# Two LSTM layers under each other, the fourth 18 steps behind instead of 19, with two gates in one sigmoid and the gate o summed apart in the last steps

## What is computed

```python
x = x + cond_layer(x)                  # x @ (base + rank-8 part of cond) + x
x = x + tanh(x @ W_ih.T + cond @ W_hh.T + b_hh + b_ih)
x = x + lstm(x, cond, L2_Wx, L2_Wh, L2_b)      # "third layer", L2 in the code
x = x + lstm(x, cond, L3_Wx, L3_Wh, L3_b)      # "fourth layer", L3 in the code

def step(h, c, xp_t):                  # xp = x @ Wx + b
    a = xp_t + h @ Wh                  # [2, 2048]
    i, f, o, g = sigmoid(a[0:512]), sigmoid(a[512:1024]), sigmoid(a[1024:1536]), tanh(a[1536:])
    c = f * c + i * g
    h = o * tanh(c)
```

## Time and profile before

| | us |
|---|---|
| median of 3 runs | 11900.81 |
| lowest, highest | 11899.27, 11900.91 |
| the profiled execution | 11900.05 |
| its span on the core | 11898.2 |

### The profile page before, as it was taken

The page is one execution under the profiler, slowest core; times in us unless marked ns, Lnnn a source line. Parts: engine busy times, 40 slices in busy tenths (PEclk is TensorE's granted clock), DMA queues, the critical chain, the costliest instruction groups (busy, mean ns, idle before and its releaser), DMA issues.

```text
span 11898.2 us, 435945 instructions
## 1 busy us (share of the span) xinstructions
PE 11828.7 (99%) x231604; PEld 2698.0 (23%) x100532; DVE 8509.1 (72%) x46342; ACT 3758.9 (32%) x24698; POOL 1418.6 (12%) x5238
## 2 busy tenths in 40 slices
PE   8999999999999999999999999999999999999999
PEld 5222222222222222222222222222222222222222
DVE  2677777777777777777777777777777777777776
ACT  2233333333333333333333333333333333333332
POOL 4011111111111111111111111111111111111110
PEclk9999999999999999999999999999999999999999
DMA  4000000000000000000000000000000000000000
GB/s 164 25 4 5 4 5 4 5 5 4 5 5 4 5 5 4 5 4 5 4 5 5 4 5 5 4 5 5 4 5 4 5 4 5 5 4 5 5 5 3
DMA packets 374546, 107.86 MB, mean 9 GB/s; under 512 B 349594, under 2 KB 357830, under 8 KB 372436
## 3 DMA queue, kind: packets, MB, share of 16 engines
q1 hardware_dynamic: 362372, 61.96, 2.8%
q0 software_dynamic: 3504, 11.56, 0.3%
q10 hardware_dynamic: 6560, 6.32, 0.2%
HBM read 62.98 MB, written 16.78 MB: 7 GB/s over the span
## 4 chain that ended last, share of the span: by engine, by line
PE 99%; DVE 0%; issue 0%; ACT 0%; POOLq 0%; POOL 0%; DVEq 0%
PE bank L80 89%; PE bank L874 7%; PE bank L518 1%; PE bank L531 1%; PE bank L484 0%; DVE gates_t L1055 0%; DVE gates_t L1062 0%; ACT gate_o L950 0%; DVE state L1085 0%; DVE state L1088 0%; DVE state L1081 0%; ACT tanh_c L952 0%; DVE pre L1068 0%; DVE pre L1061 0%; DVE g_fc L1065 0%
## 5 line engine op out<-in xcount | busy, mean ns | idle before, releaser
L80 PE MATMUL bank<-wh,state 128*6 128x512 bf16 x196608 | 11055.6, 379 | 20.8 <-DVE state L1088 20.8
L1054 DVE STREAM_TRANSPOSE gates_t<-bank 128x256 f32<-128x256 f32 x4096 | 1843.6, 450 | 2015.3 <-PE bank L80 2013.7
L80 PEld LDWEIGHTS bank<-wh,state 128*6 128x6 bf16 x65536 | 1568.1, 86 | 7400.5 <-issue 6498.0
L945 ACT ACTIVATE gate_if<-pre 128x8 f32<-128x8 f32 x4096 | 859.8, 210 | 7256.0 <-DVE pre L1059 7256.0
L1081 DVE TENSOR_TENSOR state<-gate_o,tanh_c 128x8 f32<-128x8 f32 x4096 | 688.2, 168 | 836.0 <-ACT tanh_c L952 811.2
L1062 DVE STREAM_TRANSPOSE gates_t<-bank 128x128 f32<-128x128 f32 x4096 | 1252.5, 306 | 0.0
L1055 DVE STREAM_TRANSPOSE gates_t<-bank 128x128 f32<-128x128 f32 x4096 | 1122.9, 274 | 0.0
L983 POOL TENSOR_TENSOR y<-x,state 128x8 f32<-128x8 f32 x2048 | 434.5, 212 | 5374.2 <-DVE state L1088 5374.2
L950 ACT ACTIVATE gate_o<-pre 128x8 f32<-128x8 f32 x4096 | 855.0, 209 | 642.8 <-DVE pre L1068 642.4
L983 POOL TENSOR_TENSOR x<-x1r,state 128x8 f32<-128x8 f32 x2048 | 434.5, 212 | 4961.2 <-DVE state L1088 4961.2
L952 ACT ACTIVATE tanh_c<-g_c 128x8 f32<-128x8 f32 x4096 | 854.7, 209 | 9.7 <-DVE g_c L1072 9.7
(11 more groups left out here) (124 smaller groups left out, 3490.6 us busy)
## 6 DMA issues: line engine op xcount, KB each, us to landing
w<-in_w SPq DMA_DIRECT2D x8, 2048.0 KB, 13.2
out<-y_rows SPq DMA_DIRECT2D x1020, 8.0 KB, 1.8
wx<-in_x SPq DMA_DIRECT2D x16, 512.0 KB, 5.4
x1p<-x_t_all SPq DMA_DIRECT2D x128, 64.0 KB, 2.6
x1r<-x_t_all SPq DMA_DIRECT2D x128, 64.0 KB, 2.6
x_t_all<-wx ACTq DMA_DIRECT2D x6, 1024.0 KB, 4.8
wx<-in_Wh POOLq DMA_DIRECT2D x8, 512.0 KB, 4.2
wx<-in_Wh POOLq DMA_DIRECT2D x16, 256.0 KB, 4.9
```

The source lines that it names most:

```text
L80: return pe.add_instruction(mybir.InstMatmult(name=nc.get_next_instruction_name(), engine=mybir.EngineType.PE, ins=[pe.lower_ap(moving), p ...
L945: act.activation(gate_if[l][:, 1, :, 1], pre[l][:, HB:2 * HB], ACT.Sigmoid).then_inc(S[l]["f"], 1)
L1054: dve.transpose(gates_t[l][:, 0:gf, NS * NB:], banked[:, 0:gf]).then_inc(s["trans_if"], 1)
```

## The change

It has three parts.

1. LAG is 18 instead of 19. ROWS_AT falls from 4 to 3 by its formula. In the first chunk where only the fourth layer is left (number 128), its first step of the chunk's data is now step 2, the one in which quarters 2 and 3 were turned; so `done_before` moves them to step 1 there, behind quarters 0 and 1, and GpSimd adds the biases ahead of the residual in that step, since the residual waits for the state that VectorE writes only after the turning.
2. ScalarE does the sigmoids of i and f in one activation of 16 elements; the semaphore f becomes `if`.
3. In chunks 128 and 129, where the fourth layer is alone, the matmuls are done twice over the blocks of rows: 48 of 384 columns for i, f and g into the layer's own bank, then 48 of 128 columns for o into the third layer's bank, with a semaphore mm_o for the second. VectorE transposes o from there and waits for mm_o first.

```diff
-LAG = CH + 2 + 1
+LAG = CH + 2
 ...
+        if self.number == NCH:
+            own = [(L3, -1, 2), (L3, -1, 3)]
+            found = [x for x in found if x not in own] + (own if s == 1 else [])
+        return found
+    def lone(self):
+        return self.number is not None and self.number >= NCH
+    def own_turned(self, s):
+        return self.number == NCH and s == 1
 ...
-                def matmuls(l):
-                    w = wh[l][:, :, :, :, :, :, :].rearrange("p h k j s m c -> p h k j s (m c)")
+                def matmuls(l, to=None, first=0, last=NMS):
+                    to = gates[l][:, 0:NMS * C] if to is None else to
+                    w = wh[l][:, :, :, :, :, first:last, :].rearrange("p h k j s m c -> p h k j s (m c)")
 ...
-                            matmuls(l).then_inc(S[l]["mm"], 1)
+                            if t.lone():
+                                ifg = 3 * NH // NS
+                                matmuls(l, gates[l][:, 0:ifg * C], 0, ifg).then_inc(S[l]["mm"], 1)
+                                matmuls(l, gates[L2][:, 0:NMS * C - ifg * C], ifg).then_inc(S[l]["mm_o"], 1)
+                            else:
+                                matmuls(l).then_inc(S[l]["mm"], 1)
 ...
-                            act.activation(gate_if[l][:, 1, :, 1], pre[l][:, HB:2 * HB], ACT.Sigmoid).then_inc(S[l]["f"], 1)
-                            act.activation(gate_if[l][:, 0, :, 1], pre[l][:, 0:HB], ACT.Sigmoid)
+                            act.activation(gate_if[l][:, :, :, 1], pre[l][:, 0:2 * HB].rearrange("p (w n) -> p w n", w=2),
+                                           ACT.Sigmoid).then_inc(S[l]["if"], 1)
 ...
-                            residual(l, t, s)
-                            for x in t.done_before(l, s):
-                                add_bias(x[0], t, *x[1:])
+                            if t.own_turned(s):
+                                for x in t.done_before(l, s):
+                                    add_bias(x[0], t, *x[1:])
+                                residual(l, t, s)
+                            else:
+                                residual(l, t, s)
+                                for x in t.done_before(l, s):
+                                    add_bias(x[0], t, *x[1:])
 ...
-                            dve.transpose(gates_t[l][:, ifg:, NS * NB:], banked[:, ifg:]).then_inc(s["trans_o"], 1)
-
-                            dve.wait_ge(s["f"], n)
+                            apart = banked[:, ifg:]
+                            if t.lone():
+                                apart = gates[L2][:, 0:NMS * C - ifg * C].rearrange("p (m c) -> p m c", c=C)
+                                dve.wait_ge(s["mm_o"], t.count(l, step) - NCH * CH + LAG)
+                            dve.transpose(gates_t[l][:, ifg:, NS * NB:], apart).then_inc(s["trans_o"], 1)
+
+                            dve.wait_ge(s["if"], n)
```

More of the change, by code:

```diff
@@ L678, in done_before @@
             found = [(x, d - 1, q, h) for x, d, q, h in found]
-        return [x[:3] for x in found if x[3] == NH - 1]
+        found = [x[:3] for x in found if x[3] == NH - 1]
+        if self.number == NCH:
[6 more added lines that the diff above has]
+        return self.number == NCH and s == 1
 def layers_and_recurrence(nc, ins, keep, turn, pool_stream, cut_done, x1_dram, out):
@@ L733, in blocks_of @@
             return [(NFRONT + n // (2 * NH), n // NH % 2, n % NH) for n in units]
-        names = ("mm", "xp", "trans_if", "trans_g", "trans_o", "pre_if", "pre_g", "pre_o", "f", "g", "fc", "c", "tanh", "h", "r1", "r2", "res",
+        names = ("mm", "mm_o", "xp", "trans_if", "trans_g", "trans_o", "pre_if", "pre_g", "pre_o", "if", "g", "fc", "c", "tanh", "h", "r1", "r2", "res",
                  "proj", "turn", "ready")
@@ L847, in matmuls @@
                                 for j in range(NJ):
-                                    mm = column_tile(nc, pe, gates[l][C * j:C * j + SPAN, 0:NMS * C],
+                                    mm = column_tile(nc, pe, to[C * j:C * j + SPAN, :],
                                                      placed(state[l], h, s), w[:, h, k, j, s, :], j,
```

## The result

| | before | changed |
|---|---|---|
| median of 22 runs each, us | 11900.9 | 11880.69 |
| lowest, highest | 11898.14, 11905.38 | 11879.06, 11889.79 |
| the profiled execution | 11900.05 | 11879.89 |
| its span | 11898.2 | 11878.0 |

The ratio is 0.9984, with a 95% interval of 0.9978 to 0.999. The kernel became 20.2 us (0.17%) shorter. It is at the lower edge of the range: the median lies 0.3 us under its end of 11881, while the ratio, taken of the 11900.81 that the prediction started from, gives 11881.8, just inside.

The account below looks back on a forecast made before the run. TensorE, full from 600 to 11700 us, bounds the paired stretch; a chain bounds the lone steps. End 16.7 us less, head 0.39 more, state 0.05 earlier: 16.4 less, so 11883.7 profiled, 11884.4 us median; range 11881 to 11894.

Parts of the forecast that it names:

- within 0.2%: Whole kernel: change smaller than 0.2% (24 us), chance 0.94; faster by more 0.03, slower by more 0.03.
- The lone step: The 18 last steps, fourth layer alone: 4.49 us from matmul to matmul instead of 5.18.
- the prediction's bounds: Rounds of 128-column o matmuls in the last steps: 0.056 us taken, 0.11 us at the other end.
- The merged sigmoid: Sigmoid of f and i: 0.01 us longer operation, lone chain 0.05 us shorter (0 to 0.08), paired stretch gains nothing.
- The copy of xp: Fourth layer's first step in each chunk: copy has 0.06 us to spare, 0.49 us of cover altogether, costs nothing.
- The head: Start of the kernel, where the fourth layer begins one step earlier: 0.39 us more.
- The second lone step: Fourth layer's second step alone: state 2.24 us later, behind projections and turned quarters; a stretch of about 6.7 us.
- The clock: First lone step: clock granted at 0.50 again after the idle stretch, matmuls 4.41 us instead of 2.76, 1.65 us kept.
- Rival (d): The low clock meets other steps or none: 1.65 us either way, 11882.8 or 11886; chance 0.75 together with the main forecast.
- The paired stretch: 600 to 11700 us, both layers running: TensorE full, pace kept, no other engine can shorten it, change of nothing.
- idle time of TensorE: Sign looked for: none between 600 and 11700 us; any ahead of L80 in each chunk's step 3 would disprove the forecast.

Follow-up runs that it names:

- e1_merge: The kernel before with only the sigmoids of f and i merged into one activation, LAG 19, no split: 11895.6 us, ratio 0.9996.
- e4_late2: The changed kernel with two unused 128x128 additions on GpSimd ahead of the bias addition of the fourth layer's quarter 3: 11926.13 us, ratio 1.0021.
- e5_late1: The changed kernel with one unused 128x128 addition on GpSimd ahead of the bias addition of the fourth layer's quarter 3: 11883.35 us, ratio 0.9988.
- e2_lag18: The kernel before with only the lag cut to 18 and quarters 2 and 3 of chunk 128 turned in step 1: 11897.07 us, ratio 0.9998.
- e10_own: The changed kernel with chunk 128's quarters 2 and 3 turned behind step 1's state, GpSimd's residual ahead of its biases again: 11880.31 us, ratio 0.9983.
- e6_late2_lag19: The kernel before (LAG 19) with two unused 128x128 additions on GpSimd ahead of the fourth layer's quarter 3 bias addition, run once: 11903.36 us.
- e3_split: The kernel before with only the separate sum of gate o in the lone steps, LAG 19 and two sigmoids: 11886.31 us, ratio 0.9989.
- e9_three: The changed kernel with g in a bank of its own too, scan and tanh of c ahead of o, 7 warming sets: 11878.69 us, ratio 0.9982.
- e11_three_own: The changed kernel with g in a bank of its own and the last two quarters turned behind the second lone step's state: 11876.99 us, ratio 0.9982.
- e7_warm10: The changed kernel with 10 warming sets of matmuls in a lone step instead of 8: 11889.18 us, ratio 0.999.
- e8_warm0: The changed kernel without any warming sets of matmuls in the lone steps: 11881.95 us, ratio 0.9985.

## Why the prediction came out 3.7 us high

Its mechanism held at the end of the kernel, where it saw the gain, and its forecast of "within 0.2%" held. Two terms that it put at nothing were not nothing: in the paired stretch the merged sigmoid gives 2.5 us and the shorter lag takes 1.85. That they nearly cancel is luck (one trace each). By its own terms:

**The lone step: 4.49 forecast, 4.50 measured.** The first transpose is 0.64 us earlier as worked out. The rounds come from the row of 96 matmuls, which lasts 2.79 us: the first transpose at 2.16 puts twelve rounds of 384 columns at 0.163 each, 1.96 in all, and the rest, 0.83 less the 0.219 of a last matmul, is eleven rounds of 128 columns at 0.056. That is the lower end of the prediction's bounds. The means are in the groups of TensorE from 11805 to 11870 us, with shapes apart (columns as in the earlier trace rows):

```profile
L80 PE MATMUL bank<-wh,state 128*6 128x384 bf16 x712 | 31.5, 326 | 0.0
...
L80 PE MATMUL bank<-wh,state 128*6 128x128 bf16 x672 | 11.8, 219 | 0.0
```

With four matmuls to a round they start 0.014 us apart on average. The Trainium skill, "TensorE: Matmul & The Clock Gate", Part 1, has about 25 ns as the least between two starts of matmuls back to back; here, where four column tiles run side by side, the trace does not agree. By that page the 48 matmuls of o would have taken an estimated 1.2 us. They took 0.61 and the drain, and VectorE never waited for them.

**The merged sigmoid: 0.01 more forecast, 0.010 measured** (0.220 at 16 elements, 0.210 at 8), and g begins 0.12 behind it. The chain is 0.05 to 0.06 shorter, by e1_merge. The step does nothing to a paired step's pace in itself, but see below.

**The copy of xp: 0.06 us to spare forecast, about 0.10 measured.** The timeline of a chunk's step 2, in the changed kernel:

```profile
5697.14 0.46 POOL L1012 TENSOR_TENSOR area<-turned,bias_all 128x128 f32<-128x128 f32 x1
...
5697.64 0.22 ACT L961 COPY gates_t<-area 128x32 f32<-128x32 f32 x1 [1.34 <-POOL area L1012]
...
5698.00 0.18 DVE L1084 TENSOR_REDUCE pre<-gates_t 128x16 f32<-128x64 f32 x1
```

The copy ends at 5697.86, the reduction that reads it starts at 5698.00, and the hand-over takes 0.03. Beyond that e4_late2 and e5_late1 measured the cover: 0.32 us of lateness is free, 0.72 costs 0.33 a chunk. So the cover is about 0.4 (0.43 forecast behind the reduction).

**The head: +0.39 forecast, +0.28 measured** (steps 16 to 19). The lag is sized right: alone, in e2_lag18, it costs 0.39. The merged sigmoid, which the prediction left out here, takes 0.19 off the same steps in e1_merge.

**The second lone step: 6.73 forecast, 6.84 measured.** The changed kernel's timeline:

```profile
11797.45 0.19 DVE L1101 TENSOR_TENSOR_SCAN g_c<-gate_if,g_fc 128x16 f32<-128x16 f32 x1
...
11797.90 1.95 PE L888 MATMUL bank<-wx,x 128*32 128x128 f32 x64 [1.06 <-DVE turned L1048]
...
11799.92 0.32 DVE L1048 STREAM_TRANSPOSE turned<-bank 128x128 f32<-128x128 f32 x1 [0.56 <-POOL area L1012]
11800.17 0.12 DVE L1110 TENSOR_TENSOR state<-gate_o,tanh_c 128x8 f32<-128x8 f32 x1
11800.32 0.50 POOL L1012 TENSOR_TENSOR area<-turned,bias_all 128x128 f32<-128x128 f32 x1 [0.41 <-DVE turned L1048]
...
11800.52 0.31 DVE L1117 TENSOR_TENSOR state<-state 128x8 f32<-128x8 f32 x1
...
11800.89 2.79 PE L80 MATMUL bank<-wh,state 128*6 128x384 bf16 x96 [1.04 <-DVE state L1117]
```

From the scan to the first operation of the state (L1110) it is 2.72 us, and 2.71 were forecast. The last transpose names GpSimd as what released it. That is the event that came last by the profile, but in the code this transpose waits for the projection and for the biases of quarter 1, which were done at 11798.82; the projection ended at 11799.85, and e10_own shows the same 0.07 from its end to the transpose. The 0.1 us too much arise behind that: the last subtraction takes 0.31 in place of 0.17. It runs beside an addition of GpSimd; whether that is the reason wasn't tried.

**The clock: 1.65 us forecast, nothing measured. This is the mis-sized term.** The prediction kept the low clock of the first lone step, since TensorE idles there as before. It does, 2.37 us against 2.42, but its matmuls ran at full clock, 2.79 us in place of 4.41:

```profile
11789.54 2.79 PE L80 MATMUL bank<-wh,state 128*6 128x384 bf16 x96 [2.37 <-DVE state L1117]
```

The other traces show that this changes from trace to trace. Of the eleven kernels tried, seven had the fall there or within a step of it, and e4_late2, e5_late1, e6_late2_lag19 and e10_own had none, with the same idle time. At the head it is the same. Around step 15 of the third layer, the kernel before has 0.50 and e4_late2 1.00 in the same window, after idle times of 2.21 and 2.15 us:

```profile
377.50:380.90 3.40, 3.40 (x36) 0.30 (x8) 0.00 (x0) 0.00 (x0) 0.00 (x0) 0.50 0.42 43
```

```profile
377.50:380.90 3.40, 2.49 (x48) 0.49 (x20) 0.99 (x5) 0.36 (x3) 0.21 (x1) 1.00 0.28 63
```

The first line is the kernel before, the second e4_late2. From step 15 to 16 it is 6.95 us in the kernel before and 5.20 in e4_late2. The -0.34 us between steps 15 and 16 of the changed kernel fit this too: its fall began 1.20 us behind the end of the idle time (375.78 to 376.98), in the kernel before 0.64 behind it (376.89 to 377.53). What decides whether there is a fall stays open. Rival (d) named this, at 11882.8, and is the case that came true in this trace.

**The paired stretch: nothing forecast, 1.03 us less measured.** "Nothing on VectorE, ScalarE or GpSimd can shorten the time" there was nearly right. A few of TensorE's matmuls start late, because of delays that the chain of the step let through, and with a shorter chain they start less late. The sign that the prediction looked for, idle time of TensorE, can't show them: they are mostly under the 0.16 us by which a matmul's end outlasts the next one's start. The kernel before lacks 0.72 us of busy time in the paired stretch, once, while 124 of its chunks (all but the first two and the last) are together 4.0 us above the undisturbed length, and those of the changed kernel 2.9. The section on the hardware shows them.

**The start.** 1.05 us less before the first state is no effect of the change. That state came between 269.2 and 276.5 us in the thirteen traces, without an order by kernel. Four of them (e3_split, e6_late2_lag19, e9_three, e11_three_own) have it at 273.7 or later and, with one clock fall more at the head, 1.6 us more in steps 0 to 15. Up to step 15 they are 5.0 to 7.8 us behind the changed kernel's trace, about as far as 5 of that kernel's 22 runs (11886.81 to 11889.79) lie above the other 17 (up to 11882.05). With one trace each this limits what can be told from a span.

In sum, the forecast was 16.4 us less. To it come 1.65 for the clock, 1.03 for the paired stretch, 1.10 for the start and the steps to 15, 0.34 for the clock at step 15 and 0.11 at the head; 0.30 for the lone steps go off, and 0.04 for a state that was 0.01 earlier instead of 0.05. That is 20.29 us, and the profile has 20.26. This accounts for one pair of traces. The medians are 20.2 apart as well, but 3.1 us of the sum (the clock at both ends and the start) change from trace to trace, so how they stand in the other runs isn't shown.

## What to carry to other kernels

Where one engine is full nearly the whole time, a gain of another engine's work counts only in the stretches where the chain is alone, so the sum is a number of lone steps by what a step loses; handing over a part of the sums in a bank of its own took 0.64 us out of 5.18, while the matmuls grew from 2.76 to 2.79. An idle time of nothing doesn't prove that an engine is never late: two lengths of the same stretch do. Before a lag or a buffer distance is shortened, the spare time on every queue that it moves past should be read, and how far a late operation can move before the bound engine waits: here 0.1 us to the next operation and 0.4 more to TensorE, and 0.3 us beyond that cost twice what the whole change brought. A clock fall in one profile isn't a term to carry over but a case with a chance.

## What the runs showed of the hardware that was not expected

**VectorE stands still for 0.24 to 0.37 us at fixed places of the program.** The scan of the kernel before, in the timeline:

```profile
5983.41 0.19 ACT L948 ACTIVATE g_fc<-pre 128x8 f32<-128x8 f32 x1
5983.44 0.17 DVE L1065 TENSOR_TENSOR g_fc<-gate_if,g_c 128x8 f32<-128x8 f32 x1
...
5984.07 0.19 DVE L1072 TENSOR_TENSOR_SCAN g_c<-gate_if,g_fc 128x16 f32<-128x16 f32 x1 [0.34 <-issue]
...
5985.16 0.09 PEld L80 LDWEIGHTS bank<-wh,state 128*6 128x6 bf16 x4 [0.91 <-DVE state L1088]
```

Its inputs are there (g at 5983.60, the product at 5983.61), and it waits for nothing that the profile shows. The waits view counts these (kernel before):

```profile
DVE g_c L1072 <- issue: 10.2, 30, 0.4
```

The delays come at the same chunks in each pass of the loop of 40 chunks. The lengths of single chunks, from one residual of step 0 to the next chunk's, show what reaches TensorE:

| | before | e2_lag18 | e1_merge | changed |
|---|---|---|---|---|
| a chunk without delay, us | 89.87 | 89.87 | 89.87 | 89.87 |
| delayed ones in a pass of 40 | 5 of 90.02, 4 of 89.93 | 8 of 90.02, 3 of 89.93 | 5 of 89.94 | 8 of 89.95 |
| two neighbours in each pass, together | +0.14 | +0.15 | +0.06 | +0.07 |
| the chunk where the loop ends | 90.76 | 91.12 | 90.54 | 90.95 |
| the paired stretch | 11318.18 | 11320.03 | 11315.64 | 11317.15 |

The lag sets which chunks have a delay: 8 at 18 steps, 5 at 19. The sigmoid sets what one costs: 0.15 us with the old chain, 0.07 to 0.08 with the merged sigmoid, at either lag. That its chain, shorter by 0.05 to 0.06, leaves the matmuls more room is the explanation that fits. So the merged sigmoid alone takes 2.5 us from the paired stretch, the lag alone adds 1.85, and together they take 1.0 (one trace each; of the other traces with both edits and nothing added on GpSimd, four have 11316.9 to 11317.2 and e7_warm10 11318.2). The same place in the program with the merged sigmoid, in e1_merge:

```profile
5982.45 0.19 DVE L1072 TENSOR_TENSOR_SCAN g_c<-gate_if,g_fc 128x16 f32<-128x16 f32 x1 [0.26 <-issue]
...
5983.54 0.09 PEld L80 LDWEIGHTS bank<-wh,state 128*6 128x6 bf16 x4 [0.83 <-DVE state L1088]
```

Where the loop ends there is a longer one, once, in the kernel before:

```profile
11449.25 0.17 DVE L1065 TENSOR_TENSOR g_fc<-gate_if,g_c 128x8 f32<-128x8 f32 x1 [1.97 <-issue]
```

The chunk with it takes 90.76 us in the kernel before, 91.12 in e2_lag18, 90.54 in e1_merge and 90.95 in the changed one.

The traces tie these places to the fetching of instructions. The page of the kernel before lists a DMA queue for them (packets, MB, share of the engines' span):

```profile
q14 instruction: 800, 6.55, 0.2%
```

Between 600 and 11400 us VectorE stands still for no visible reason 51 times in the kernel before and 60 times in the changed one. In the trace's record of packets a packet of 8192 bytes starts in this queue 0.5 to 1.1 us behind the end of each of these 111 pauses; behind a moment taken at random one does so within 1 us in 7 of 100 cases. Around the long pause at the loop's end one packet starts 1.7 us ahead of its end and one 0.7 behind. What in the fetching holds VectorE stays open, and no run changed it.

**The full clock survives long idle shares.** In e8_warm0, behind a fall in the first lone step, TensorE was busy for 63% of the stretch from 11795 to 11870 us, idle for 1.70 us ahead of each step, and the granted clock stayed at 1.00 throughout, in the one trace of it. In all the traces of both kernels and the experiments, a fall to 0.50 came only behind idle times of 2.1 us and more or within a step of one, and there not always. The warming matmuls had seemed to be what keeps the clock; in the lone steps of this trace they weren't needed.
